# A fourth product tap on ScalarE and GpSimd, wider side columns, and casting and accumulating DMAs in a fused two-layer convolution kernel

## What is computed

```
# layer 0
g  = group_norm(x)                                  # 32 groups, per image
xh = einsum('bchw,oc->bohw', g, w_in) + b_in        # 128 -> 256 channels
h  = relu(mean(xh, (2, 3)) @ kg_w1.T + kg_b1)
k  = (h @ kg_w2.T + kg_b2).reshape(b, 256, 3, 3)    # a 3x3 kernel per image and channel
y  = depthwise_conv3x3(xh, k, padding=1)
y  = y * tanh(softplus(y))                          # mish
x  = x + einsum('bchw,oc->bohw', y, w_out) + b_out  # 256 -> 128
# layer 1: FFT over channels, mask, two 128x128 maps, inverse FFT, real part, relu
x  = x + relu(real(ifft(maps(fft(group_norm(x))))))
```

## Time and profile before

| | us |
|---|---|
| median of 3 runs | 3897.72 |
| lowest, highest | 3897.64, 3898.21 |
| the profiled execution | 3897.35 |
| its span, first to last instruction | 3895.3 |

### The profile page before, as it was taken

The page is one execution under the profiler, slowest core; times in us unless marked ns, Lnnn a source line. Parts: engine busy times, 40 slices in busy tenths (PEclk is TensorE's granted clock), DMA queues, the critical chain, the costliest instruction groups (busy, mean ns, idle before and its releaser), DMA issues.

```text
span 3895.3 us, 65845 instructions
## 1 busy us (share of the span) xinstructions
PE 3759.3 (97%) x22348; PEld 2259.9 (58%) x22348; DVE 3525.0 (90%) x4778; ACT 3448.4 (89%) x5604; POOL 2632.5 (68%) x2132
## 2 busy tenths in 40 slices
PE   4899999999999999999999999999999999999998
PEld 2555655656555555555556555565655556556554
DVE  5899989899998989989899898998989899899996
ACT  4988999898998989989899998999989999898875
POOL 3456676776767767677777767767677776777763
PEclk8999999999999999999999999999999999999999
DMA  3112333333233333333333332333333233231223
GB/s 139 64 46 85 109 108 110 103 109 114 98 114 103 109 109 105 113 104 109 103 112 111 104 110 102 112 111 103 109 104 113 105 109 111 103 113 71 74 73 124
DMA packets 111292, 401.86 MB, mean 103 GB/s; under 512 B 13232, under 2 KB 14320, under 8 KB 110704
## 3 DMA queue, kind: packets, MB, share of 16 engines
q1 hardware_dynamic: 110960, 397.66, 29.5%
HBM read 263.39 MB, written 134.22 MB: 102 GB/s over the span
## 4 chain that ended last, share of the span: by engine, by line
PE 77%; ACT 7%; POOL 4%; issue 3%; DVE 2%; ACTq 0%; POOLq 0%
PE psA L657 35%; PE psBO L703 19%; PE psL L712 9%; PE psBO L681 2%; PE psBO L683 2%; PE psBO L682 2%; ACT tprod L413 2%; POOL tsum L1110 2%; PE psBO L692 1%; ACT XS L454 1%; PE psBO L694 1%; PE psBO L693 1%; ACT xh L386 1%; PE psA L666 1%; DVE accS L924 1%
## 5 line engine op out<-in xcount | busy, mean ns | idle before, releaser
L657 PE MATMUL psA<-hi,wa 128*128 128x288 f16 (+4 forms) x9792 | 1938.6, 280 | 0.8 <-DVE wtmp L881 0.8
L912 DVE SCALAR_TENSOR_TENSOR accB<-xh,vectors,accB 128x1024 f32<-128x1024 f32 x1280 | 1640.1, 1281 | 0.0
L1110 POOL TENSOR_TENSOR tsum<-tsum,tprod 128x1024 f32<-128x1024 f32 x512 | 1210.6, 2364 | 315.9 <-ACT tprod L413 315.9
L924 DVE SCALAR_TENSOR_TENSOR accS<-side,vectors,accS 128x448 f32<-128x448 f32 x2048 | 1398.6, 683 | 24.1 <-ACT accS L422 14.9
L657 PE MATMUL psA<-lo,wa 128*128 128x288 f16 (+5 forms) x4896 | 1322.0, 280 | 0.0
L657 PEld LDWEIGHTS psA<-hi,wa 128*128 128x128 f16 x9792 | 926.8, 98 | 328.7 <-issue 63.0
L703 PE MATMUL psBO<-wm,woutt 128*128 128x512 f32 x2048 | 963.2, 593 | 3.6 <-DVE X L934 2.1
L1114 POOL TENSOR_TENSOR X<-X,zt 128x512 f32<-128x512 f32 x480 | 612.4, 1276 | 464.3 <-DVE accB L912 394.7
L1102 POOL TENSOR_TENSOR lo<-X,hi 128x1024 f16<-128x1024 f32 x256 | 547.6, 2139 | 359.2 <-ACT hi L371 356.9
L703 PEld LDWEIGHTS psBO<-wm,woutt 128*128 128x128 f32 x2048 | 386.5, 190 | 482.4 <-issue 481.0
L413 ACT ACTIVATE tprod<-xh,vectors 128x1024 f32<-128x1024 f32 x512 | 583.6, 1140 | 31.4 <-POOL tsum L1110 29.4
(11 more groups left out here) (166 smaller groups left out, 3434.6 us busy)
## 6 DMA issues: line engine op xcount, KB each, us to landing
X<-in_x_dram SPq DMA_DIRECT2D x256, 512.0 KB, 3.3
out_dram<-X SPq DMA_DIRECT2D x256, 512.0 KB, 2.6
XS<-in_x_dram SPq DMA_DIRECT2D x240, 512.0 KB, 3.3
X<-in_w_t_dram SPq DMA_DIRECT2D x2, 1152.0 KB, 17.6
w1t<-in_w_t_dram SPq DMA_DIRECT2D x1, 256.0 KB, 2.8
wint<-in_w_in_t_dram SPq DMA_DIRECT2D x1, 128.0 KB, 2.3
woutt<-in_w_out_t_dram SPq DMA_DIRECT2D x1, 128.0 KB, 2.8
wm<-in_cos_m_dram SPq DMA_DIRECT2D x1, 64.0 KB, 4.1
```

What stands on the lines that cost most here:

```text
L657: last = mm(o[:, r:r + q, 0:cols], w, src[:, at:at + q, SIDE + dx - 1:SIDE + dx - 1 + cols], start=(tap == ORDER[0] and w is wh and src is ...
L912: V.scalar_tensor_tensor(out=rows_of(accB[:]), in0=xh[:, 8 * j + dy:8 * j + dy + 8, dx:dx + W], scalar=kk[i % 2][:, TAPS + k:TAPS + k + 1] ...
L924: V.scalar_tensor_tensor(out=side_out(), in0=side[:, 8 * j + dy:8 * j + dy + 8, dx:dx + SIDE], scalar=kk[i % 2][:, k:k + 1], in1=side_out( ...
L1110: P.tensor_tensor(tsum[:], tsum[:], tprod[:], ALU.add).then_inc(s_ta, 1)
```

## The change

1. EXTRA 2 -> 3: ScalarE makes four products of the upper half's taps, GpSimd three adds, VectorE five taps.
2. SIDE 56 -> 63: each convolution matmul has 4 x 65 = 260 columns, each side product 8 x 64 = 512, each side tap 8 x 63 = 504.
3. `hi` is no longer written by ScalarE's cast, but by a DMA that GpSimd issues from x in DRAM, which rounds to float16, three strips ahead instead of two (`high`).
4. GpSimd's `add` is no longer an operation on X, but a DMA with accumulation from zt to the output in DRAM. SP stores a strip as soon as its residual is made.
5. On VectorE, the residual of strip n - 2 moves behind the second tap and the first side tap. The low half's subtraction (`cast`) moves to the end of GpSimd's slot. The parameter steps of the next image start one slot earlier.

```
-SIDE = 56
-EXTRA = 2
+SIDE = 63
+EXTRA = 3
...
             def store(m):
...
-                eng.wait_ge(s_add, 2 * m + 2)
+                eng.wait_ge(s_x1, 2 * m + 2)
...
         @block.scalar
...
-                if n + 2 < N:
-                    cast(n + 2)
...
-                    for k in range(2, EXTRA + 1):
-                        tap_product(n + 1, k)
+                    tap_product(n + 1, 2)
                 for c in stats[0:1]:
                     squares_x(c)
+                if n + 1 < N:
+                    tap_product(n + 1, 3)
...
         @block.vector
...
                 tap(n, 1)
-                if n >= 2:
-                    residual(n - 2, 1)
+                tap(n, 2)
+                side_tap(n, 1)
...
+                if n >= 2:
+                    residual(n - 2, 1)
...
         @block.gpsimd
...
+            def high(n):
+
+                b, s, j = n // STRIPS, n % STRIPS, n % 4
+                if n >= 3:
+                    eng.wait_ge(s_cv, 2 * (n - 3) + 1)
+                if n >= 4:
+                    eng.wait_ge(s_xm, 3 * (n - 4) + 3)
+                    eng.wait_ge(s_lo, n - 3)
+                eng.dma_start(hi[:, 8 * j:8 * j + 8, :].rearrange("p r c -> p (r c)"),
+                              x[b, :, s * SP:(s + 1) * SP]).then_inc(s_hi[j], 16)
...
                 eng.wait_ge(s_re, 2 * m + t + 1)
-                P.tensor_tensor(half(m, t), half(m, t), zt[:, t, :], ALU.add).then_inc(s_add, 1)
+                eng.wait_ge(s_out[m % 4], 16 * (m // 4 + 1))
+                eng.dma_start(out[b, :, at:at + TP], zt[:, t, :], accum_op=ALU.add).then_inc(s_acc[t], 16)
```

More of the change, by code:

```diff
@@ L141, in conv_preact_kernel @@
         s_valid = sem("s_valid")
-        s_hi = sem("s_hi")
+        s_hi = [sem(f"s_hi{j}") for j in range(4)]
         s_lo = sem("s_lo")
@@ L159, in conv_preact_kernel @@
         s_re = sem("s_re")
-        s_add = sem("s_add")
+        s_acc = [sem(f"s_acc{t}") for t in range(2)]
         s_b0 = sem("s_b0")
@@ L284, in _ @@
             for n in range(N):
-                if n >= LAG1 + 1:
-                    store(n - LAG1 - 1)
+                if 3 <= n < N - STRIPS + 3:
+                    store(n - 3)
                 if STRIPS <= n + 3 < N:
@@ L291, in _ @@
                         load_stat(c + 1)
-            for m in range(N - LAG1 - 1, N - STRIPS):
-                store(m)
             for s in range(STRIPS):
@@ L302, in _ @@
             eng.wait_ge(s_sin, 16 * STATS)
+            for t in range(2):
+                eng.wait_ge(s_acc[t], 16 * (N - STRIPS))
         @block.scalar
@@ L484, in _ @@
             eng.wait_ge(s_zero, 5)
-            cast(0)
-            cast(1)
             stats_group("x", 0, small_bank(0))
@@ L505, in slot @@
                 build = b < B - 1
-                if s == 10 and build:
+                if s == 9 and build:
                     moments("x", b + 1)
@@ L962, in slot @@
                 tap(n, 1)
-                if n >= 2:
-                    residual(n - 2, 1)
-                if s == 11 and build:
+                tap(n, 2)
+                side_tap(n, 1)
+                if s == 10 and build:
                     root_bits("x", b + 1)
@@ L968, in slot @@
                     root_bits("1", b - 1)
-                side_tap(n, 1)
-                if s == 11 and build:
+                if n >= 2:
+                    residual(n - 2, 1)
+                if s == 10 and build:
                     root_first("x", b + 1)
@@ L973, in slot @@
                     root_first("1", b - 1)
-                tap(n, 2)
                 side_tap(n, 2)
-                if s == 14 and build:
-                    tap_matrices(b + 1, 0, small_bank(1))
-                if s == 15 and build:
-                    tap_matrices(b + 1, 2, small_bank(1))
                 tap(n, 3)
@@ L985, in slot @@
                 side_tap(n, 5)
-                if s == 14 and build:
-                    tap_matrices(b + 1, 1, small_bank(0))
-                tap(n, 6)
-                side_tap(n, 6)
+                if s >= 13 and build:
+                    tap_matrices(b + 1, s - 13, small_bank(0))
                 if n >= 1:
                     residual(n - 1, 0)
+                side_tap(n, 6)
                 side_tap(n, 7)
@@ L1135, in slot @@
                 b, s, m = n // STRIPS, n % STRIPS, n - LAG1
+                build = b < B - 1
                 eng.wait_ge(s_tap, NB * n + 1)
@@ L1139, in slot @@
                     add(m - 1, 1)
-                if n + 2 < N:
-                    cast(n + 2)
-                build = b < B - 1
                 if s == 12 and build:
-                    pool_bias(b + 1)
+                    hidden_low(b + 1)
+                    weights_halves(b + 1)
                 if s == 13 and build:
@@ L1147, in slot @@
                 if s in (14, 15) and build:
-                    taps_halves(b + 1, 0 if s == 14 else 2)
+                    taps_halves(b + 1, s - 14)
                 if n + 1 < N:
                     tap_add(n + 1, 1)
+                if n + 3 < N:
+                    high(n + 3)
+                if s == 11 and build:
+                    pool_bias(b + 1)
                 if m >= 0:
@@ L1155, in slot @@
                         tap_add(n + 1, k)
+                if n + 3 < N:
+                    cast(n + 3)
+                if s == 9 and build:
+                    variance("x", b + 1, s_px)
                 if s == 10 and build:
-                    variance("x", b + 1, s_px)
-                if s == 11 and build:
                     rstd("x", b + 1, s_px)
                     fold(b + 1)
-                if s == 12 and build:
-                    hidden_low(b + 1)
-                    weights_halves(b + 1)
-                if s == 14 and build:
-                    taps_halves(b + 1, 1)
+                if s == 15 and build:
+                    taps_halves(b + 1, 2)
                 if s == 1 and b >= 1:
```

90 lines of the change are left out of this document (42 added, 48 removed).

## The result

The changed kernel takes 5129.56 us, the median of 4 runs from 5125.55 to 5130.06; the kernel before, run beside it, takes 3897.97 (3897.64 to 3899.13). The ratio is 1.3157, with a 95% interval from 1.3134 to 1.3179: slower by 32%. Forecast were 5267 us and a range from 4650 to 5490. The profiled execution took 5130.06 us for a span of 5128.3.

A forecast was written before the change was run, and what follows sets the result against it. A loop of waits among ScalarE, GpSimd and VectorE was to bind, not busy time. Start 77, 19 x 19.2 = 365, 236 x 19.8 = 4673, images 75, end 75: span 5265, plus 2 gives 5267 us; range 4650 to 5490.

The forecast's parts named there:

- The ring: Loop per strip through add 3, subtraction, first tap, residual, squares and product-add rounds: 19.2 us without DMA issue delay.
- the issue's delay: Two DMA issues on GpSimd between adds 1 and 2 delay add 2 by 2x - 1.40: 0.6 us, loop 19.8.
- The start and the end: Time before the first side product, 77 us, and after the last, 75 us.
- the DMA issue on GpSimd: GpSimd's time to issue one DMA, not in the trace: taken as 1.0 us, between 0.33 and 1.28.
- the images: Once-per-image work (root chain, layer 1 moments, pooled bias, bias rows): 5 us an image, 75 in all.
- The single tile: All products pass through tprod, so each next product waits for the previous add: 3.74 us a round.
- the steps 5 and 6: Loop parts from product 1 to 2, next product at 15.44 us, and from 2 to 3, 3.74 through add 2.
- the tap comes first: Rival: VectorE's first tap gets ahead of GpSimd's subtraction; loop 17.9 us, 4785 us in all; chance 0.18.
- The signs in the profile: Expected waits: squares 3.7 us, product 3 2.2, GpSimd before add 1 6; first tap 3.2; TensorE 75% busy.
- a rival (5780 us): Rival: waiting TensorE drops to half clock; loop 21.8 us or more; chance 0.11, shared with an issue far above 1.3.
- The dearer form: In the slower-TensorE rival, the convolution also runs at half clock, making ScalarE's mish up to 2 us late.
- Columns and DMAs: TensorE's 13.6 us a strip and the DMAs' landing, apart from two issues, taken as hidden within 19.8 us.

The follow-up runs named there:

- experiment 1: Changed kernel with GpSimd's low-half subtraction put back behind its wait for VectorE's first tap: 4754.3 us.
- experiment 2: Changed kernel with VectorE's residual of strip n - 2 put back right behind the first tap: 4782.0 us.
- experiment 7: Changed kernel with both orders of before (subtraction, residual) put back and a second product tile, ring of x 22 strips instead of 23: 4029.8 us.
- experiment 3: Changed kernel with both the subtraction and the residual put back in their places of before: 4564.9 us.
- experiment 6: Changed kernel with two product tiles instead of one and the ring of x at 22 strips instead of 23: 4670.8 us.
- experiment 5: Changed kernel with 16 unread matmuls of 512 columns in front of TensorE's side product: 5144.0 us in one run.
- experiment 4: Kernel of experiment 3 with 12 unread matmuls of 512 columns ahead of each side product on TensorE: 4452.5 us.

## Why the prediction held, and where it was off

**The ring** held step by step. Counted from product 3 at 2352.77, add 3 ends at 3.63 (forecast 3.63), the tap at 6.80 (6.85), the residual starts at 8.68 (8.76), the squares at 9.47 (9.61), and the next product 3 comes at 19.16 (19.2 without the issue's delay). Product 1 to 2 takes 3.76 (3.75), 2 to 3 3.84 (3.74). Experiments 1 and 2, and 7 against 3, each cut the ring at one place, and each cut shortened it.

**The start and the end**: 77.2 us up to the first side product (77), 75.5 behind the last (5128.3 - 5052.8; forecast 75).

**The mis-sized term** is the DMA issue on GpSimd. The prediction took 1.0 us for each; the casting load takes 0.61, the accumulating DMA 0.90, together 1.51 instead of 2.0. By the formula of the prediction the delay of add 2 is 1.51 - 1.40 = 0.11 instead of 0.6, 0.49 less on 236 strips: 116 of the 137 us by which the forecast was too high. (In the strip shown, add 2 starts 0.01 us after it could.) The rest are ordinary strips at 19.17 instead of 19.3, some 33 us, against 12 more for the images, at 5.8 us instead of 5: (5052.78 - 77.22) - 255 x 19.17 = 87 us for 15 of them. The lower bound of the issue, SP's 0.33, and the upper, 1.28, did enclose it. The Trainium skill, "DMA: Bandwidth & Descriptors", Latency and other measured facts, gives about 1 us for the first byte of such a DMA because of the emission; the instruction on GpSimd is shorter, by these rows.

**The single tile.** Of the ring's parts that were tried, the products' single tile was the dearest: 535 us with the orders right (experiment 7; 6 holds two effects). In the prediction it was in the steps 5 and 6 and had no price of its own.

**The first tap.** The subtraction won in 253 of 256 strips, by 0.07 us. The rival "the tap comes first" gave 4785 for the case that it had lost, experiment 1 made that case and took 4754. That these are 31 us apart is partly luck. The rival's price for a strip was right, 1.89 us against 1.84 in ordinary steps, but it was counted on all 255, 482 us in place of the 375 gained, and this error of 107 us met the 137 by which the forecast itself was too high. The rival would have needed a load that takes over 7 us to land, and the casting one took 4.1. In experiment 6, where the load of x did come late, it came true in most strips. (The Trainium skill, "SBUF — State Buffer", SBUF: two separate sides, has the rule that a VectorE operation with two SBUF inputs and a GpSimd operation that reads SBUF shut each other out for a whole instruction, and the first to start wins. The rows agree, 3.12 us against 1.29, and the taps that read accB in PSUM stay at a mean of 1.29, also beside a running GpSimd operation.)

**The signs in the profile.** GpSimd was idle for 4.9 us ahead of add 1 (about 6 forecast), product 3 waited 1.9 (2.2), the tap took 3.12 (3.2), add 2 started 1.4 behind add 1's end (2), TensorE was busy for 79% (75). The squares waited 2.2 us instead of 3.7. That is no gap in the ring: in the strip shown ScalarE waits the missing part a little earlier, 0.64 for the side product and 1.02 for layer 1, since TensorE is at its lower clock there. The prediction had put that clock into a rival (5780 us) instead of into the forecast. What decided was its own sum: side product, layer 1 and output product at half clock would end at about 8.3, just before the residual at 8.76; the output product makes way for the convolution at 7.74 (2360.51), and the residual starts at 8.68. In experiment 5, with the clock nearly back, there was nothing to gain. The dearer form, a convolution at half clock too, did not come: its matmuls start 0.11 us apart from the first on.

**Columns and DMAs.** Beyond the start and the end and the two issues, the prediction took them as hidden in the ring. With the ring taken away they are gains: 46 us for 60 columns, 45 for the DMAs with the earlier parameter steps.

**Where my theory fell short** was behind the prediction. For experiments 3, 4 and 7 I expected 4200 to 4250, 4200 and 3800 us and got 4565, 4452 and 4030. Two terms were missing or too small: the lower clock, once it is no longer covered (112 us), and the strips with parameter work (87 us in the changed kernel, but 186 in experiment 1, 168 in experiment 4 and 186 in experiment 7). Which of their steps decides there was not settled.

## What to carry to other kernels

Busy shares say what the time could be, not what it will be: ahead of handing an engine more work, draw the ring of waits that it closes and add up one turn, with every instruction that stands on the same queue between two of its steps. Where two engines hand one tile back and forth, a second tile was worth more (535 us) than either order alone; and an instruction off the path, moved to where it starts 0.07 us ahead of one on the path, cost 375. A change of several parts should be run part by part: here the DMAs and the wider side columns were a gain of 2.0% together (2.3% with 60 columns), under a fourth product and two orders that cost 1310 us.
